# Rest rows of two attentions as 32-row tiles, gate weights as one operand, and a new written-out order

## What is computed

```python
x = x + xattn0(layernorm(x), ctx)   # 8 heads of 64; q, k, v, softmax over 154 keys, Wo, bo
x = x + ffn0(layernorm(x))          # shared SwiGLU of 128 + 16 experts of 64; sigmoid gate, 2 of 4 groups, top 4
x = x + xattn1(layernorm(x), ctx)   # 16 heads of 8; same form, no bias
x = x + ffn1(layernorm(x))          # shared SwiGLU of 256 + 8 experts of 256; router + bias, top 2
```

## Time and profile before

| | us |
|---|---|
| median of 3 runs | 264.98 (264.64 to 266.26) |
| the profiled execution, its own time | 264.93 |
| its span, first to last instruction | 263.0 |
| TensorE busy | 247.1 (94%) |
| VectorE busy | 179.6 (68%) |
| ScalarE busy | 164.6 (63%) |
| GpSimd busy | 120.9 (46%) |

### The profile page before, as it was taken

The page is one execution under the profiler, slowest core; times in us unless marked ns, Lnnn a source line. Parts: engine busy times, 40 slices in busy tenths (PEclk is TensorE's granted clock), DMA queues, the critical chain, the costliest instruction groups (busy, mean ns, idle before and its releaser), DMA issues.

```text
span 263.0 us, 4617 instructions
## 1 busy us (share of the span) xinstructions
PE 247.1 (94%) x1360; PEld 186.4 (71%) x1360; DVE 179.6 (68%) x485; ACT 164.6 (63%) x395; POOL 120.9 (46%) x108
## 2 busy tenths in 40 slices
PE   1999999999999989999689999999999999999993
PEld 1578893965589878789466566466887878888872
DVE  5789992488446774599848793565486766567673
ACT  2789999854449694650238655996456685554651
POOL 4404669194019594794400000122779263681830
PEclk9999999999999999999959999999999999999998
DMA  7850000000069605900500000001600009000002
GB/s 220 271 196 2 2 0 0 4 0 2 0 141 331 216 0 120 205 1 4 179 5 1 2 0 7 0 4 56 265 4 0 0 10 314 1 0 0 2 0 80
DMA packets 7318, 17.41 MB, mean 66 GB/s; under 512 B 1516, under 2 KB 2350, under 8 KB 6912
## 3 DMA queue, kind: packets, MB, share of 16 engines
q1 hardware_dynamic: 7072, 16.81, 21.0%
q10 hardware_dynamic: 224, 0.32, 0.4%
HBM read 16.44 MB, written 0.62 MB: 65 GB/s over the span
## 4 chain that ended last, share of the span: by engine, by line
PE 82%; DMA 7%; ACT 4%; DVE 2%; issue 2%; SPq 2%; POOL 0%; ACTq 0%; POOLq 0%
PE psum L1040 12%; PE psum L1042 12%; PE psum L1041 12%; DMA w_src<-in_w 5%; PE psum L1156 4%; PE psum L1093 4%; PE psum L1209 3%; PE psum L1163 3%; PE psum L1164 3%; PE psum L1219 3%; PE psum L1165 3%; PE psum L1191 3%; PE psum L1103 3%; PE psum L1224 3%; PE psum L1107 3%; PE psum L1063 3%
## 5 line engine op out<-in xcount | busy, mean ns | idle before, releaser
L620 POOL TENSOR_TENSOR act_s<-act_s,spread 128x512 f32<-128x512 f32 x48 | 60.8, 1293 | 34.7 <-ACT act_s L713 27.3
L1040 PE MATMUL psum<-xT_hi,w_hi 128*128 128x512 f32 x108 | 44.6, 413 | 0.8 <-ACT act_s L713 0.8
L1042 PE MATMUL psum<-xT_hi,w_lo 128*128 128x512 f32 x108 | 42.6, 395 | 0.0
L1041 PE MATMUL psum<-xT_lo,w_hi 128*128 128x512 f32 x108 | 42.5, 393 | 0.0
L713 ACT ACTIVATE act_s<-psum 128x512 f32<-128x512 f32 x54 | 31.0, 597 | 15.9 <-PE psum L1042 10.9
L578 POOL TENSOR_TENSOR rstd<-vareps,minus_half 128x4 f32<-128x4 f32 x8 | 8.1, 1011 | 62.0 <-DVE vareps L814 62.0
L891 DVE TENSOR_TENSOR q<-psum,q 128x512 fp32r<-128x512 f32 x36 | 24.7, 689 | 14.7 <-ACT q L722 14.6
L722 ACT CAST q<-psum 128x512 fp32r<-128x512 f32 x36 | 21.0, 587 | 18.6 <-PE psum L1165 16.3
L600 POOL TENSOR_TENSOR prob_n<-prob,row_inv 128x1024 f32<-128x1024 f32 (+1 forms) x16 | 19.1, 1223 | 21.2 <-DVE row_inv L867 15.8
L988 DVE TENSOR_TENSOR psum<-psum,act_s 128x512 f32<-128x512 f32 x36 | 24.3, 692 | 5.7 <-PE psum L1042 3.0
L1009 DVE TENSOR_REDUCE neg_max<-psum 128x2 f32<-128x308 f32 x64 | 26.1, 470 | 2.4 <-PE psum L1191 2.3
(11 more groups left out here) (151 smaller groups left out, 531.4 us busy)
## 6 DMA issues: line engine op xcount, KB each, us to landing
spread<-cw SPq DMA_DIRECT2D x16, 256.0 KB, 5.9
spread<-cw SPq DMA_DIRECT2D x8, 512.0 KB, 5.2
w_src<-in_w SPq DMA_DIRECT2D x2, 1152.0 KB, 5.8
w_src<-in_w SPq DMA_DIRECT2D x1, 2304.0 KB, 13.3
w<-in_w SPq DMA_DIRECT2D x1, 576.0 KB, 8.0
X<-in_x SPq DMA_DIRECT2D x2, 256.0 KB, 4.3
wq_src<-in_wq SPq DMA_DIRECT2D x2, 256.0 KB, 4.6
out<-X SPq DMA_DIRECT2D x2, 256.0 KB, 2.0
```

The lines of the kernel that those rows point to most:

```text
L620: pool.tensor_tensor(g, g, spread[:, slot, :], ALU.mult).then_inc(weighed, 1)
L1040: pe.matmul(dst, w_hi, m_hi, start=True, stop=False)
L1041: pe.matmul(dst, w_hi, m_lo, start=False, stop=False)
L1042: return pe.matmul(dst, w_lo, m_hi, start=False, stop=True)
```

## The change

Parts: (1) the rest rows of the first attention are a step `rest` of their own for each batch, before its `pv` steps: eight matmuls over 32 rows each, into the four banks of the four `pv`; `vs0` shrinks to the rest values without zeros; (2) the same in the second attention, `rest1`: sixteen 32 x 32 tiles for four groups; `expT` with j = 4 becomes `expR` with a buffer `rest_exp` of its own; (3) `vs` and `vs1` are one step for both batches, made of column tiles, and `ctxT_rest` and `vs0_mask` are not loaded any more; (4) the gate's high and low weights lie side by side and are one operand; DVE adds the two parts; (5) new orders for PE, ACT, DVE and POOL. SP's order is the same.

```diff
-    for kind in ("vf", "vs", "wo", "bo"):
+    for kind in ("vf", "rest", "wo", "bo"):
+    steps.append(("vs",))
...
+    steps += [("rest1", b, h) for b in batches for h in range(len(REST_SETS))]   # one set: (0, 1, 2, 3)
+    steps.append(("vs1",))
...
-                vs0 = sb("vs0", [P, B, PAIRS, P], F32, r2)
+                vs0 = sb("vs0", [P, B, P], F32, r2)
-                vs1 = sb("vs1", [P, B, G1, P], F32, r2)
+                vs1 = sb("vs1", [P, B, G1, PAD], F32, r2)
-                probT1 = sb("probT1", [P, 2, 5, TOK], F32, r2)
+                probT1 = sb("probT1", [P, 2, 4, TOK], F32, r2)
+                rest_exp = sb("rest_exp", [P, G1, TOK], F32, r2)
...
-        N_CONST, N_CTX, N_CTXV, N_WQKV1 = 8, 2, 2, 8
+        N_CONST, N_CTX, N_CTXV, N_WQKV1 = 7, 2, 1, 7
-            load(ctxT_rest[0:CD, :, :], a["ctxT_rest"][0:CD, :, :], "ctxv")
-            load(ctxT_rest[CD:CD + 1, :, :], a["ctxT_rest"][CD:CD + 1, :, :], "wqkv1")
...
 POOL, norm (the rest part) and place_k1s
+                    inv = row_inv[:, b, t, :].rearrange("p (q j) -> p j q", j=2).unsqueeze(3).broadcast_to((P, 2, PAIRS, REST))
+                    pool.tensor_tensor(rest[:, r, :, :, 0:REST], prob[:, r, :, P:CTX].rearrange("p (q j) c -> p j q c", j=2),
+                                       inv, ALU.mult).then_inc(prob_normed, 1)
+                    for at, heads in ((slice(0, 4 - g), slice(g, 4)), (slice(4 - g, 4), slice(0, g))):
+                        n = heads.stop - heads.start
+                        if n:
+                            rows = head_rows[:, heads].unsqueeze(1).unsqueeze(3).broadcast_to((P, B, n, PAD))
+                            ins = pool.tensor_tensor(k1s[:, :, g, at, :], k.broadcast_to((P, B, n, PAD)), rows, ALU.mult)
 ACT
-                    wait_filled(act, step)
-                    act.activation(g["e"], g["logit"], ACT.Exp, scale=-1.0).then_inc(gate_exp, 1)
+                    act.wait_ge(logit_ready, step[2] + 1)
+                    act.activation(g["logit"], g["logit"], ACT.Exp, scale=-1.0).then_inc(gate_exp, 1)
+                elif kind == "expR":
+                    b, g = step[1:]
+                    wait_filled(act, step)
+                    if b == 1:
+                        act.wait_ge(rest1_summed, len(REST_SETS))
+                    moved(act.activation(rest_exp[:, g, :], bank(step), ACT.Exp, scale=HEAD_SCALE1), step)
 DVE
+                elif kind == "vs":
+                    wait_filled(dve, step)
+                    moved(dve.tensor_copy(vs0[:, :, :], bank(step)[:, 0:B * P].rearrange("p (b c) -> p b c", b=B)), step)
+                elif kind == "vs1":
+                    chain(dve.tensor_reduce(real_rows[:, :], vs1_mask[:, :], AX, ALU.max))
+                    moved(dve.tensor_scalar(vs1[:, :, :, :].rearrange("p b g c -> p (b g c)"), bank(step)[:, 0:B * P],
+                                            real_rows[:, 0:1], None, ALU.mult), step)
+                elif kind == "gate":
+                    summed = dve.tensor_reduce(g["logit"].rearrange("p t (k e) -> p (t k) e", e=8), g["raw"], AX, ALU.add)
+                    if s == 1:
+                        summed.then_inc(logit_ready, 1)
 PE, vs and vs1
+                        for b in range(B):
+                            for r in range(4):
+                                rows, at = slice(PAD * r, PAD * r + PAD), b * P
+                                if kind == "vs":
+                                    parts = [w[:, r * P:(r + 1) * P]]
+                                else:
+                                    heads = w[:, :].rearrange("k (h c) -> k h c", c=PAD)
+                                    parts = [heads[:, r:G1 * (4 - r):5, :], heads[:, G1 * (4 - r):H1:5, :]][:1 + (r > 0)]
+                                for part in parts:
...
+                                    ins = pe.matmul(dst, ctxT[0:k, b, P:CP], part, start=True, stop=True,
+                                                    skip_group_check=True, tile_position=(0, PAD * r))
 PE, rest (new) and pv
+                    for j in range(2):
+                        for p in range(PAIRS):
+                            rows, cols = slice(PAD * p, PAD * p + PAD), slice(64 * j, 64 * j + 64)
+                            pe.matmul(bank(("pv", b, p))[cols, :], vs0[rows, b, cols], probT0[rows, H0 + j, :],
+                                      start=True, stop=False, skip_group_check=True, tile_position=(PAD * p, 64 * j))
-                    for j in range(2):
-                        pe.matmul(bank(step)[64 * j:64 * j + 64, :], vs0[:, b, p, 64 * j:64 * j + 64], probT0[:, H0 + p // 2, :],
-                                  start=True, stop=False, skip_group_check=True)
 PE, gate
-                        ins = product3(bank(step)[:, t * n_e:(t + 1) * n_e], xT_hi[:, b, x], xT_lo[:, b, x],
-                                       gates_hi[:, c], gates_lo[:, c])
+                        pe.matmul(dst, xT_hi[:, b, t * P:(t + 1) * P], both, start=True, stop=False)
+                        ins = pe.matmul(dst, xT_lo[:, b, t * P:(t + 1) * P], both, start=False, stop=True)
 PE, rest1 (new) and pv1
+                    wait_moved(pe, ("vs1",))
+                    for g in REST_SETS[h]:
+                        wait_bank_free(pe, ("pv1", b, g))
+                        wait_moved(pe, ("expR", b, g))
+                    for g in REST_SETS[h]:
+                        for r in range(4):
+                            rows, j = slice(PAD * r, PAD * r + PAD), (r + g) % 4
+                            ins = pe.matmul(bank(("pv1", b, g))[PAD * j:PAD * j + PAD, :], vs1[rows, b, g, :], rest_exp[rows, g, :],
+                                            start=True, stop=False, skip_group_check=True, tile_position=(PAD * r, PAD * j))
+                    ins.then_inc(rest1_summed, 1)
-                    for j in range(4):
-                        pe.matmul(bank(step)[rows, :], vs1[:, b, g, rows], probT1[:, r, 4, :], start=True, stop=False,
-                                  skip_group_check=True, tile_position=(0, PAD * j))
```

More of the change, by code:

```diff
@@ L78 @@
 ROUTE_PARTS = {1: 4, 3: 2}
+REST_SETS = ((0, 1, 2, 3),)
 ROW_PARTS = (slice(0, CD), slice(CD, CD + 1))
@@ L114, in all_steps @@
     steps += [("place_k1", g, j) for g in groups for j in range(4)]
-    for kind in ("vf1", "vs1", "mT", "onT", "wo1"):
+    for kind in ("vf1", "mT", "onT", "wo1"):
         steps += per_batch(kind)
+    steps += [("rest1", b, h) for b in batches for h in range(len(REST_SETS))]
+    steps.append(("vs1",))
     for kind in ("q1", "pv1", "oT"):
@@ L119, in all_steps @@
     steps += [("score1", b, t, g, half) for b in batches for t in range(T) for g in groups for half in range(2)]
-    steps += [("expT", b, g, j) for b in batches for g in groups for j in range(5)]
+    steps += [("expR", b, g) for b in batches for g in groups]
+    steps += [("expT", b, g, j) for b in batches for g in groups for j in range(4)]
     steps += per_sublayer("store", (1, 3)) + [("spread", s, b, c) for s in (1, 3) for b in batches for c in range(SLOTS // 2)]
@@ L186 @@
     "Pool":
[L187 to L190 removed]
+        "lnA split lnA bo split norm norm norm norm split norm split norm norm lnA norm bo split lnA split " +
@@ L191 @@
+        "place_k1s " + 6 * "weigh " +
+        "place_k1s weigh weigh split lnA weigh weigh weigh weigh weigh split place_k1s split weigh weigh " +
+        "weigh split split split lnA place_k1s split lnA split split weigh weigh weigh lnA " + 29 * "weigh ",
     "SP":
@@ L204, in takes @@
     if kind == "gate":
-        return (engine == "ACT") == (step[1] == 1)
+        return engine == "DVE" or step[1] == 1
     if kind == "route":
@@ L223, in bank_uses @@
     for step, token in zip(order_of("PE"), PROGRAM["PE"].split()):
-        if "." in token:
-            bank = int(token.split(".")[1])
+        kind, banks = step[0], [int(k) for k in token.split(".")[1:]]
+        if kind == "rest":
+            keys = [("pv", step[1], p) for p in range(PAIRS)]
+        elif kind == "rest1":
+            keys = [("pv1", step[1], g) for g in REST_SETS[step[2]]]
+        else:
+            keys = [("y",) + step[1:3] if kind == "down" else step]
+        for key, bank in zip(keys, banks):
             count[bank] = count.get(bank, 0) + 1
-            uses[("y",) + step[1:3] if step[0] == "down" else step] = (bank, count[bank])
+            uses[key] = (bank, count[bank])
     return uses
@@ L1045, in _ @@
                 kind = step[0]
-                if step in uses:
+                if step in uses and kind not in ("pv", "pv1"):
                     wait_bank_free(pe, step)
```

191 lines of the change are left out of this document (98 added, 93 removed), and 56 rows, old and new, of the table PROGRAM.

## The result

| | before | after |
|---|---|---|
| median | 264.86 us (264.64 to 266.26, 4 runs) | 256.27 us (255.79 to 257.04, 4 runs) |
| ratio, 95% interval | | 0.9682 (0.9647 to 0.9717) |
| profiled execution, its span | 264.93 us, 263.0 us | 255.82 us, 253.4 us |
| TensorE busy | 247.1 us | 234.3 us |

The account below looks back on a forecast made before the run. TensorE, busy 94% of the span, was taken as the bound: 18.99 us removed less 6.27 added gives 12.72 net, less 1.7 not coming through is 11.0 off 264.93, forecast 254.0 us, range 249 to 261.

Parts of the forecast that it names:

- What the change removes and adds on PE: Rests, rest values and gates: 18.99 us of PE removed, 6.27 added, net 12.72 us.
- A microsecond of matmul is a microsecond of the total: In PE's full stretches, matmul time removed comes off the total, unless another engine is as full there.
- (a): Up to the first rest, ACT and DVE nearly without a gap: 0.4 of PE's 1.0 us comes through, 0.6 lost.
- what does not come through: Whole kernel: part of PE's net 12.7 us cut not reaching the total, 1.7 us lost.
- the new order of the start: Start, xT before kT steps, values later: scores wait for ACT, so nothing, between -1 and +1 us.
- (b): Gates: the added reduce's hop to ACT before the exp, 0.3 us lost.
- (c): From 126 us on: fetch of the maxima and first exp of batch 1 show more, 0.8 us lost.
- The forecast's signs of being wrong: Rest blocks of several us; PE idle over 2 us within 20-60 or 139-182 us; a second half-clock stretch, or none.
- half stays with the neighbours: Attentions: ACT, DVE, banks or new waits keep half, 5.5 us lost instead of 1.4; about 258 us; chance 0.15.
- the clock: Half-clock stretch of 6.8 us behind PE's hole: gone, 250.5 us, chance 0.10; one more such stretch, 257.4 us, chance 0.05.
- four at a time: At most four tiles run side by side, so rest1 costs four blocks, rest two; 260.6 us; chance 0.05.
- tiles of one bank take turns: Rest1: row tiles writing one bank take turns, 13.8 us instead of 0.97; 279.6 us; chance 0.05.

Follow-up runs that it names:

- experiment 5: Kernel after with all matmul savings undone (rests, gates, rest values), its new orders, steps, copies and buffers kept: 268.66 us, ratio 1.0162.
- experiments 1 to 4: Kernel after, one saving undone each: first attention's rest over all rows 260.60 us; second's 261.72; gates as three matmuls 256.93; rest values by full calls 258.25.
- experiment 4: Kernel after with the rest values of each layer made by two full matmuls as before: 258.25 us, ratio 0.9735.
- Experiments 7 to 9: Kernel after plus unread matmuls in TensorE's hole behind the first FFN: eleven 255.18 us; four, early only, 255.34; seven, early only, 254.56.
- experiment 6: Kernel after with the small rest tiles issued inside each pv and pv1, not all together: 270.42 us, ratio 1.0202.
- experiment 8: Kernel after with four unread matmuls before vf1(1), in TensorE's hole behind the first FFN, none before xT(2,1): 255.34 us, ratio 0.9638.
- experiments 9 and 8: Kernel after with unread matmuls before vf1(1) only, none before xT(2,1): seven 254.56 us, ratio 0.9596; four 255.34 us, ratio 0.9638.

## Why the prediction was right, and where it was off

The range (249 to 261) and the sign held; the time was 2.3 us above the forecast.

- *What the change removes and adds on PE: right to within a microsecond.* 12.72 us net were forecast, busy time fell by 12.8. That close it is in part luck: against the new orders with all savings undone busy time fell by 13.8, and those orders have 1.0 more of it than the kernel before (experiment 5). Rest 1.04 and 1.12 us (forecast 1.06), rest1 1.15 (1.20 with its way out; the first score1 behind it takes 0.34 us instead of 0.14, so 1.35). The joint vs takes 0.57 us and about 0.2 behind it (0.73 forecast). vs1 was too dear in the forecast: its records and the next start lie 0.63 us apart (54.30 to 54.93), forecast 1.25.
- *A microsecond of matmul is a microsecond of the total: nearly right*, the point on which the most hung. Given back together, 13.8 us of TensorE's busy time cost 12.4 us by the medians and 12.9 by the profiled executions. The parts alone cost 4.3, 5.4, 0.7 and 2.0 us, where the chain and the starts give 4.8, 5.0, 1.8 and 2.0 (experiments 1 to 4); the gates come out lowest, in a run that is not clean.
- *(a) of what does not come through* (0.6 us, ScalarE and VectorE full up to the first rest): the first pv block came at 39.03 us before and the first rest at 38.23 after, 0.8 us earlier. That looks like 0.8 of the 1.0, but three scores (1.3 us) had moved from before it to behind it, and TensorE had 2.4 us less busy time up to there (32.8 to 30.4). So 1.6 were lost, not 0.6, all of it idle time in the first 20 us. Two terms are in it. With the full values in the new order (the edit of experiment 4 or 5) the first rest comes at 39.11 or 39.16, so 0.9 of 1.3 us pass, and (a) itself is about 0.4. The rest is the new order of the start, which the forecast put at "nothing, between -1 and +1": it cost more, about 1.4 us by experiment 5.
- *(b), the gate hops* (0.3): no wait of `cwT` stands among TensorE's waits. Nothing lost.
- *(c), from 126 us on* (0.8): 1.1 were lost behind VectorE's add. The size was near, the cause was another. In the hole TensorE's idle time fell from 3.6 to 3.3 us, and none of its waits names the fetch of the maxima. The new waits are behind the hole: 0.85 us of a score1 for VectorE's q (134.44), 0.34 of the first rest1 for a maximum, 0.64 of an `xT` for xn (163.24); the kernel before had 0.16 and 0.32 us between its last q1 and its second FFN.
- *The step that was off* is the term "what does not come through", 1.7 us, which measured 12.8 - 8.6 = 4.2 (3.7 by the two profiled executions). What it left out is the new orders as such. They were priced by what is full and by single edits, while the lists of all four engines were new: five waits of `xT` for xn instead of two (4.4 us against 1.9, 1.4 of the 2.5 more in the start), and k1's wait of 0.9 us at 52.5 us, which in VectorE's list lies behind a stalled instruction. Undoing all matmul savings and keeping the rest gives 268.7 us, about 4 us above the kernel before, 2.4 of them idle time of TensorE and 1.0 busy time. What of this the joint steps made unavoidable stays open. The forecast's signs of being wrong did not catch it: from 20 to 60 us and from 134 to 175 us (139 to 182 before) TensorE was idle for 1.1 and 1.6 us, under the 2 us named, and no sign looked at the first 20 us.
- *Rival "half stays with the neighbours"* (258): its size is near, its cause is refuted. If neighbours kept half, giving the work back would cost half its length; it cost 12.4 to 12.9 of 13.8 us.
- *Rival "the clock"*: neither vanished nor doubled; the stretch of 6.8 us at half clock stood before and after. Experiments 7 to 9 show what it was worth: about 2.4 us of the 3.4 that the count gives.
- *Rivals "four at a time" and "tiles of one bank take turns"*: refuted, 16 tiles in 1.15 us.

The Trainium skill ("TensorEngine Tiling (Array Packing)", Restrictions and Gotchas, PSUM Pressure) says that different row tiles cannot use one PSUM bank at the same time. Here four row tiles that write one bank, each in its own 32 partitions, overlap fully (0.99 us with a border, experiment 6). Where page and measurement differ the measurement decides: in this form it is no bound. The Trainium skill's factor of 10.6 for 16 tiles ("TensorE: Matmul & The Clock Gate", Part 3) gave an estimate of 1.3 us; measured were 1.15 with the border before it, 12 times less than 16 x 0.86.

## What to carry to other kernels

A matmul over few rows costs as much as a full one unless others run beside it: gather row and column tiles from several steps into one block, and count the block once. A saving on a full engine passed nearly one to one, but a new order had a price of its own; measure it by undoing the savings and keeping the order, before the neighbours are blamed. When two orders are compared at a landmark, count what each has done by then, and look at the start of the kernel too. Keeping an idle stretch busy paid here through the clock of what followed (254.56 us against 256.27, with matmuls that nothing reads), with work that ended before the awaited operand was there. Real work moved into it gained nothing, as it left a hole where it came from.

## What was not expected of the hardware

- Sixteen 32 x 32 float32 tiles of 512 columns, four of them in each bank, in 1.15 us, only 0.16 us more than four tiles (0.99).
- A TENSOR_SCALAR of VectorE on 128 x 4 elements took 1.20 and 1.88 us instead of 0.17 while GpSimd multiplied 128 x 1024 elements (1.90 us), and ended with it. The Trainium skill ("SBUF — State Buffer", Terms, shared port pair) states that the two engines take turns at one pair of ports and that the loser waits for the whole instruction; these two rows agree. No run here tries another form of the small instruction.
- The clock behind the hole differs between executions of one kernel: a mean of 0.993 four times and 0.984 twice in experiment 8, which is about 3.4 or 6.8 us at half clock (read in the profiled executions of experiments 9 and 8), and the second kind took 1.0 us longer on average (256.05 against 255.07).
